# Adjacency blocks built in two pairs of PSUM banks in turn, attribute products in one pair and one quad later

## What is computed

```python
edge_input = jnp.concatenate([x[src], edge_attr], axis=-1)
messages = _gelu(edge_input @ mW1 + mb1) @ mW2 + mb2
gates = jax.nn.sigmoid(_gelu(edge_input @ gW1 + gb1) @ gW2 + gb2)
aggregated = jax.ops.segment_sum(messages * gates, dst, num_segments=x.shape[0])
```

```python
msg = norm[:, None] * h[row]
out = jax.ops.segment_sum(msg, col, num_segments=n)
```

## Time and profile before

| | us |
|---|---|
| median of 3 runs | 11216.09 |
| lowest, highest | 11200.21, 11229.92 |
| the profiled execution | 11224.96 |
| its span from the first to the last instruction | 11223.1 |
| PE busy | 8285.4 |
| POOL busy | 6745.8 |
| DVE busy | 5185.2 |
| ACT busy | 2896.1 |
| mean granted TensorE clock | 0.85 |

### The profile page before, as it was taken

How to read it: one execution, slowest core, us unless ns; L and a number is a source line. 1 busy time by engine, 2 the same in 40 slices (tenths; PEclk the granted TensorE clock), 3 DMA queues, 4 the chain that set the end, 5 groups by cost and what they waited for, 6 DMA issues and landing times. The chain is left out here.

```text
span 11223.1 us, 161106 instructions
## 1 busy us (share of the span) xinstructions
PE 8285.4 (74%) x40104; PEld 5619.5 (50%) x40104; DVE 5185.2 (46%) x17514; ACT 2896.1 (26%) x6502; POOL 6745.8 (60%) x6696
## 2 busy tenths in 40 slices
PE   5567667676666667766758888888876888888886
PEld 4334444444444444444445655556554555555554
DVE  5566666666666666666622222222222222222223
ACT  4345555555555555555400000000000000000000
POOL 4665555565655565666456666666655666666663
PEclk7688888888888888888768998888887888888887
DMA  4345555565655566666447767677665676766666
GB/s 152 81 130 169 169 170 168 171 174 168 173 167 172 168 173 171 171 172 173 136 147 234 239 228 233 228 235 240 222 201 181 229 235 228 236 233 228 233 225 200
DMA packets 1329031, 2149.86 MB, mean 192 GB/s; under 512 B 306427, under 2 KB 1079948, under 8 KB 1328700
## 3 DMA queue, kind: packets, MB, share of 16 engines
q10 hardware_dynamic: 142400, 986.64, 24.7%
q1 hardware_dynamic: 925996, 684.95, 20.8%
q0 software_dynamic: 260560, 477.49, 15.9%
HBM read 1587.45 MB, written 560.99 MB: 191 GB/s over the span
## 5 line engine op out<-in xcount | busy, mean ns | idle before, releaser
L927 POOL DMA_INDIRECT hid<-conv_table,hid x3452 | 3389.3, 982 | 1962.6 <-issue 1031.5
L883 POOL DMA_INDIRECT hid<-src_table,src_ids x3127 | 3174.7, 1015 | 2115.5 <-ACT msg L1255 1127.1
L1137 PE MATMUL bd<-ring,table_sb 128*96 128x280 f32 x13720 | 3618.3, 421 | 307.3 <-issue 245.0
L1137 PEld LDWEIGHTS bd<-ring,table_sb 128*96 128x96 f32 x13720 | 2341.8, 173 | 1501.4 <-issue 647.2
L1033 PE MATMUL bd<-one_hot_dst,one_hot_src 128*128 128x343 bf16 x8400 | 1753.8, 353 | 1463.7 <-ACT blocks L1263 1193.1
L1033 PEld LDWEIGHTS bd<-one_hot_dst,one_hot_src 128*128 128x128 bf16 x8400 | 840.9, 108 | 2270.9 <-issue 1811.0
L1263 ACT ACTIVATE blocks<-bd 128x686 f32<-128x686 f32 x1400 | 1116.9, 798 | 2289.4 <-remote 1503.7
L1841 DVE TENSOR_TENSOR acc<-acc,sg 96x64 f32 x434 | 94.7, 218 | 2956.3 <-remote 1568.4
L1123 PE MATMUL sg<-conv_hot,hid 128*96 128x64 f32 x6944 | 774.9, 258 | 618.4 <-issue 466.1
L1123 PEld LDWEIGHTS sg<-conv_hot,hid 128*96 128x96 f32 x6944 | 746.1, 176 | 707.7 <-issue 622.5
L1368 ACT ACTIVATE side_out<-bd,side_flag 96x280 f32<-96x280 f32 x70 | 34.3, 490 | 4015.9 <-PE bd L1137 2436.3
(11 more groups left out here) (208 smaller groups left out, 5412.3 us busy)
## 6 DMA issues: line engine op xcount, KB each, us to landing
ring<-adjacency ACTq DMA_DIRECT2D x980, 980.0 KB
adjacency<-blocks SPq DMA_DIRECT2D x700, 686.0 KB
hid<-conv_table,hid POOLq DMA_INDIRECT x3452
attr<-in_attr SPq DMA_DIRECT2D x392, 128.0 KB
hid<-src_table,src_ids POOLq DMA_INDIRECT x3127
conv_table<-table_sb SPq DMA_DIRECT2D x28, 336.0 KB, 4.7
feat_half<-feat_keep SPq DMA_DIRECT2D x56, 168.0 KB
buf_h<-dinv_rows SPq DMA_DIRECT2D x56, 168.0 KB
```

What stands on the lines that cost most here:

```text
L883: pool.indirect_dma_start(out=hid[s][:, t, :], out_offset=None, in_=src_rows, in_offset=bass.IndirectOffsetOnAxis(ap=src_ids[s // 2][:, j: ...
L927: pool.indirect_dma_start(out=conv_g[b][:, t, :], out_offset=None, in_=conv_rows[l], in_offset=bass.IndirectOffsetOnAxis(ap=conv_ids[j][:, ...
L1137: op = nc.tensor.matmul(side_ps, table_sb[:, D * k:D * (k + 1)], ring[slot][:, :, QUAD_FANS * b:QUAD_FANS * (b + 1)], start=(k == 0), stop ...
```

## The change

`build_block` writes block t into `pb` when t is even and `bd` when it is odd, and `keep_block` reads it there. `EVAC_CREDIT` is 2, so build t waits for copy t - 2. The attribute products lose `pb`: all use `pa`. They come one quad later in PE's order, the product of quad s + 2 at the start of quad s, and wait for `s_added` at 4n + s, the add of quad s - 1. The first iteration of a pass issues two products ahead and not three. Numbers and shapes of all instructions stay.

```diff
--- before.py
+++ after.py
@@ -107,7 +107,7 @@
 ROUNDER = 12582912.0
 CONV_SPARED = [min(GROUP - 1, max(0, PAD_TILES - GROUP * b)) for b in range(STEP_GROUPS)]
 SEG_CREDIT, ACC_CREDIT, SIDE_CREDIT = 3, 2, 1
-BUILT_CREDIT, EVAC_CREDIT, EATEN_CREDIT, OUT_CREDIT = SLOTS, 1, RING, 1
+BUILT_CREDIT, EVAC_CREDIT, EATEN_CREDIT, OUT_CREDIT = SLOTS, 2, RING, 1
 
 SLICES = 5
 SLICE = SIDE_TILES // SLICES
@@ -331,7 +331,7 @@
         bd = ps("bd", 1024)
         px, const = bd[:, 0:512], bd[:, 512:1024]
         iota, gate_w2_now = iota_now[:, :], gate_w2[:, :]
-        attr_ps = [pa, pb]
+        attr_ps, block_ps = pa, [pb, bd]
         table_ps = [px[:, 0:4 * D], const[:, WINDOW + D:WINDOW + 4 * D]]
         gate_ps = own_ps = px[0:D, 0:HALF]
         side_ps = const[0:D, 0:FANS].rearrange("r (q z) -> r q z", q=UNIT_QUADS)
@@ -1017,32 +1017,32 @@
                 if s % 2 == 0:
                     pe.wait_ge(s_attr[s // 2], 16 * n + 16)
                 if free:
-                    pe.wait_ge(s_added, QUADS_PER_ITER * n + s - 1)
+                    pe.wait_ge(s_added, QUADS_PER_ITER * n + s)
                 for h in range(2):
                     last = nc.tensor.matmul(
-                        attr_ps[s % 2][:, 512 * h:512 * h + 2 * H2], attr[s // 2][:, P * (s % 2):P * (s % 2 + 1)],
+                        attr_ps[:, 512 * h:512 * h + 2 * H2], attr[s // 2][:, P * (s % 2):P * (s % 2 + 1)],
                         w_attr[:, 2 * H2 * h:2 * H2 * (h + 1)], start=True, stop=True)
                 last.then_inc(s_attr_mm, 1)
 
             def build_block(t, nb):
                 y, z = y_s[t % SLOTS], z_s[t % SLOTS]
                 pe.wait_ge(s_yz, nb * OCTET + (t + 1))
-                pe.wait_ge(s_evac, nb * OCTET + (t + EVAC_CREDIT))
+                pe.wait_ge(s_evac, nb * OCTET + (t + EVAC_CREDIT - 1))
                 for h in range(2):
                     for k in range(3):
-                        op = nc.tensor.matmul(bd[:, 512 * h:512 * h + HALF_Z], y[:, 1 + k, :],
+                        op = nc.tensor.matmul(block_ps[t % 2][:, 512 * h:512 * h + HALF_Z], y[:, 1 + k, :],
                                               z[:, Z_PAD * h:Z_PAD * h + HALF_Z], start=(k == 0), stop=(k == 2))
                 op.then_inc(s_built, 1)
 
             def edges(it, n, first, last, build):
                 if first:
-                    for s in range(3):
-                        attr_product(n, s, s == 2)
+                    for s in range(2):
+                        attr_product(n, s, s > 0)
                 for s in range(QUADS_PER_ITER):
-                    if s + 3 < QUADS_PER_ITER:
-                        attr_product(n, s + 3, True)
+                    if s + 2 < QUADS_PER_ITER:
+                        attr_product(n, s + 2, True)
                     elif not last:
-                        attr_product(n + 1, s + 3 - QUADS_PER_ITER, True)
+                        attr_product(n + 1, s + 2 - QUADS_PER_ITER, True)
                     if build:
                         build_block(2 * s, build[1])
                     pe.wait_ge(s_gated, QUADS_PER_ITER * n + s + 1)
@@ -1262,7 +1262,7 @@
                 act.wait_ge(s_built, nb * OCTET + (t + 1 + BUILT_CREDIT))
                 nc.scalar.activation(
                     blocks[h][:, :, FAN * t4:FAN * (t4 + 1)].rearrange("p (h b) d -> p h b d", h=2),
-                    bd[:, :].rearrange("p (h z) -> p h z", h=2)[:, :, 0:HALF_Z].rearrange(
+                    block_ps[t % 2][:, :].rearrange("p (h z) -> p h z", h=2)[:, :, 0:HALF_Z].rearrange(
                         "p h (b d) -> p h b d", d=FAN), ACT.Copy).then_inc(s_evac, 1)
 
             def edges(it, n, first, last, build):
@@ -1538,7 +1538,7 @@
                 dve.wait_ge(s_gath[s], gathered(it, QUAD, QUAD_SPARED[s]))
                 dve.wait_ge(s_attr_mm, i + 1)
                 pair = hid[s][:, :, :].rearrange("p (b t) f -> p b (t f)", b=2)
-                v.tensor_tensor(pair, attr_ps[s % 2][:, :].rearrange("p (b c) -> p b c", b=2)[:, :, 0:2 * H2], pair,
+                v.tensor_tensor(pair, attr_ps[:, :].rearrange("p (b c) -> p b c", b=2)[:, :, 0:2 * H2], pair,
                                 ALU.add).then_inc(s_added, 1)
 
             def dot(n, s, first):
```

## The result

| | before | changed |
|---|---|---|
| median, 4 runs each | 11218.94 us | 11353.35 us |
| lowest to highest | 11200.21 to 11229.92 | 11333.8 to 11364.78 |
| ratio, 95% interval | | 1.012 [1.01, 1.014] |
| profiled execution, its span | 11223.1 us | 11350.4 us |
| mean granted TensorE clock | 0.85 | 0.833 |

The change makes the kernel 1.2% slower, 134 us. The time lies in the range given and on the side of rival C; the likeliest case, 11226, did not come true. The chip decides much about this kernel. I call a chip fast where it takes 9196 or 9197 us, and slow elsewhere. A trace of the kernel before exists only from the executions at 11219 us.

The account below looks back on a forecast made before the run. A chain of waits, hanging on the release (the copy that starts late after a store), sets the pace, no full engine. -117 + 117 + 0 + 10 = +10 us on 11216.09 gave 11226 us; range 11015 to 11375.

Parts of the forecast that it names:

- rival C: Whole kernel slower: late PE completions hit an add or even copy without slack; 11280 to 11419 us, point 11323, chance 0.27.
- the likeliest case: Whole kernel: gain and price cancel to some 0.3 us an iteration; 11170 to 11280 us, chance 0.38.
- Step (1): Build stretch: even block's build leaves the released copy's path; gain 0.33 us a half, 117 us, ends 18 and 252.
- Step (2): Build stretch: lower clock and later completions, (a) and (b) together; price 117 us, ends 0 and 308.
- (a): PE stands until weighing ends, so sum, odd build and product meet the low clock more often; 0.33 us a half.
- (b): Between store and next copy: even build completes deeper into time after store; at most 2.2 / 4 us a half.
- Step (3): DVE's add: product one quad later comes 1.7 us late, hidden under the wait for tanh; 0, at most 595 us.
- Step (4): The 21 iterations without builds, before 668 us: the product now lies between two adds; cost 10 us.
- Step (5): SP's queue: load waits for a product issued a quad later, store stands behind it; 0 us. POOL no bound yet.
- two points of decision: rival C decides once DVE's late add exceeds its 3.45 us tanh wait, or even build ends some 2 us after store.
- B: Whole kernel faster: slow even build off the path, clock unchanged; about 11045 us, 10964 to 11099, chance 0.30.
- within 27.0 to 27.6: Sign: an iteration with builds stays within 27.0 to 27.6 us; under 26.7 would mean B.

Follow-up runs that it names:

- the second execution: The changed kernel run again with no edit, beside the kernel before at 11194.2 us: 11347.84 us, ratio 1.0133.

## Why the prediction was right and wrong

- **What bounds the kernel**: right in the main reading. The copies stand still for completions and not for want of banks: PE's wait for the copy went and the time didn't. Wrong was the cause. "After a store PE's completion reaches the others late" is true in time, and the kernel without stores shows that the store isn't what delays it. Of the two readings that I left open, late signal or late execution, the add beside the released copy shows that the signal is late, by at least some 1.4 us.
- **Step (1), the gain**: 117 us forecast, 0.33 us a half. The table gives 0.31 us an iteration, 54 us, and for the second execution 13.52 - 12.38 = 1.14 us, 200 us, if the kernel before stood there as at 11219 us, of which there is no trace. Both lie within the ends of 18 and 252. The release was followed by the even copy as forecast: 2.48 and 2.86 us became 1.97 and 2.07 (means over 175 iterations), 1.3 us an iteration. But 1.1 us of that were given back before the next odd copy (2.93 and 3.01 became 3.49 and 3.57 us), since that build waits for the weighing and the sum.
- **Step (2), the price**: this is the term that was mis-sized. 117 us taken, 0.97 x 175 = 170 us measured, and with the same reservation 1.82 x 175 = 319 us in the second execution, against ends of 0 and 308. (a) was right in kind: clock 0.82, and products of quads 0 and 2 at a mean of 2.21 us in place of 1.74 and 1.59. The even copy starts 0.49 us an iteration later behind the store, 0.22 us of it because its build ends later and 0.27 us because the completion comes later, as (b) had it. That is half of the 0.97. The other half (b) gave no reader: the odd block. Block 1's build ends 1.0 us earlier (1.11 us after copy 0 in place of 2.08) and its copy starts 0.8 us later, 5.09 us after copy 0 in place of 4.28. For block 5 the copy came 0.3 us nearer, 5.14 in place of 5.48, though its build ends 0.6 us earlier. I had worked the gain out as if the release kept its distance from what PE does; half of the released copies now start 7.85 to 8.2 us after the store (195 of 349, before 56).
- **Step (3), products later**: by the rows right while blocks are built, but the hint under the block pairs speaks against a cost of exactly 0. DVE's add waits 552.9 + 249.2 us, its wait for tanh shrank from 999.9 to 410.3, and gelu waits 21.6 us for the add, before 1.7.
- **Step (4), the stretch without builds**: 10 us taken, 34 measured. I bounded it by a small number on PE's side and named no cover. There is none there: gelu waits straight for the add. The gelu and add groups of both kernels, 200 to 660 us, before and then changed:

```profile
L1242 ACT ACTIVATE hid<-hid 128x768 f32<-128x768 f32 x73 | 61.5, 843 | 148.5 <-issue 95.6 <-DVE hid L1541 53.0
...
L1541 DVE TENSOR_TENSOR hid<-pb,hid 128x768 f32<-128x768 f32 x37 | 35.3, 953 | 55.2 <-DMA hid<-src_table,src_ids 37.1 <-remote 16.5 <-issue 1.7
L1541 DVE TENSOR_TENSOR hid<-pa,hid 128x768 f32<-128x768 f32 x36 | 34.3, 952 | 50.1 <-DMA hid<-src_table,src_ids 33.6 <-remote 10.7 <-issue 5.9
```

```profile
L1541 DVE TENSOR_TENSOR hid<-pa,hid 128x768 f32<-128x768 f32 x70 | 66.9, 956 | 198.7 <-remote 152.6 <-PE pa L1022 18.9 <-DMA hid<-src_table,src_ids 16.1
...
L1242 ACT ACTIVATE hid<-hid 128x768 f32<-128x768 f32 x70 | 59.0, 843 | 241.8 <-DVE hid L1541 187.6 <-issue 54.0
```

- The add waits 152.6 us for "remote" instead of 27.2, gelu 187.6 us for the add instead of 53.0. From the second iteration on, by the starts of quad 0's adds, the mean iteration went from 24.89 to 26.34 us; 1.45 x 20 = 29 us. On a fast chip it is 21.42 us with the changed kernel and 21.41 with block pairs and early products, so this price too hangs on the slow chips.
- **Step (5), queues**: I named 0.6 us, and SP now waits much longer, but no store comes later for it (0.3 us behind the last copy, before 0.3 to 0.4). The answer to the earlier trace rows, changed kernel, 700 to 5590 us:

```profile
SPq L645 <- PE pa L1022: 130.8, 40, 9.0
SPq L645 <- remote: 66.8, 73, 2.7
```

- **The sum** with what was measured: -54 + 170 + 34 - 19 (after the last copy, which no step had) = +131 us, against 127.3 between the spans.
- **The rivals**: C's range holds the time (11280 to 11419, its point 11323). Of its two points of decision the first was not passed in the build stretch: the late add stayed under its cover. The second, an even build that ends over 2 us after the store, was passed in 187 of 349 halves, before in 2; the means, 1.2 and 1.4 us, hide it. In these halves the release comes 7.79 (block 1) and 7.58 us (block 5) after the store, in the others 7.08 and 6.77. But it was passed as often, in 172 halves, with the block pairs alone, which cost nothing measurable. In the stretch without builds C's late add is what happened. B fell, as the clock didn't stay and the release didn't keep its distance. Of what I named as signs, the iteration "within 27.0 to 27.6" failed. The copies' waits for "remote" fell from 1503.7 to 1318.9 us and not by hundreds more, and release to next copy became 1.97 and 2.07 us, near the 1.9 forecast. That the best guess of 0.1% came out as 1.2% has its measure in two terms: the gain at half its size, the prices at 1.5 and 3.4 times theirs.
- The Trainium skill's rule in "Perfetto Trace Analysis" (Matmuls), that independent matmul groups should rotate through banks, gives by my estimate some 10050 us. The trace disagrees: measured are 11353, and no difference on the chips without late completions. The Trainium skill's "TensorE: Matmul & The Clock Gate" (A second HAM failure mode) says that cycling through PSUM banks with short idle times of PE makes its clock swing. The trace agrees: the clock fell from 0.86 to 0.82. With the block pairs alone, at 0.82 too, the time was the same within 0.3%, which that section doesn't foresee.

**Open**: what holds PE's completions back on some chips (the stores are out, the gathers untested), and whether the 1.2 to 1.3% need both parts or only the chips on which the changed kernel was tried at 11200 us. Each part alone cost nothing measurable on a chip at 11472 us, but both together were not run there, and neither part alone at 11200 us. So how the loss arises in the build stretch is read from the order of time and not shown by an experiment; that the 34 us ahead of it belong to the late products is shown.

## What to carry to other kernels

Before adding a second buffer, ask whether the wait for the first one ends in what sets the pace anyway; then little is to be gained. Here the wait for the copy and the new wait for the weighing both end in the same released copy. Before a buffer's slack is moved from one user to another, look for the cover of the one who gives it in every stretch in which it runs: the products had DVE's wait for tanh while blocks were built, and nothing in the 21 iterations ahead. Look at more than a mean where a time can fall into two groups: the even build's end behind the store did. And see on more than one chip what bounds a kernel whose waits name no instruction.

## What was not expected of the hardware

- The same kernel takes 9196 and 9197 us on two chips and 11194 and 11472 us on two others. On the first two the copies wait for no "remote" releaser, in the changed kernel the odd build's end is followed by its copy in 0.7 us instead of 3.7 to 4.4, and its clock over the run is 0.94 instead of 0.83. The convolutions differ too: from the last copy to the end the changed kernel takes 4892 us on a fast chip and 5766 on the slow one.
- On the slow chips two completions of PE, 1.3 us apart by the modelled ends, reach ACT and DVE within 0.06 us of each other, 3.7 us after the first (the rows at 3011.73 and 3011.79). The signals are held and then come together.
- In the changed kernel 195 of 349 released copies start 7.85 to 8.2 us after the store's issue, and yet in the kernel before without stores, on another chip, the waits for "remote" stay at 1550 us.
